# A decoder block with a mixture of experts on one core: the first half's turned blocks laid over the normalised tokens, seven expert numbers in one word, results added in place and the last transfers on two queues

## The reference, cut to what matters

```python
def _moe(x, gate, expert_bias, w1, w2, w3, shared_w1, shared_w2, shared_w3):
    scores = jax.nn.sigmoid(xt @ gate.T)                # 896 tokens, 8 experts
    _, sel = jax.lax.top_k(scores + expert_bias, 2)     # two experts for a token
    order = jnp.argsort(sel.reshape(-1), stable=True)
    ...
    xb = (xt[token_idx] * scores_sorted[:, None]).astype(jnp.bfloat16)
    for e in range(8):
        h = jax.nn.silu(xb @ w1e.T) * (xb @ w3e.T)      # 512 -> 256
        oe = h @ w2e.T                                  # 256 -> 512
        out_r = out_r + jnp.where((expert_ids == e)[:, None], oe, 0.0)
    hs = jax.nn.silu(xt @ shared_w1.T) * (xt @ shared_w3.T)
    out = (hs @ shared_w2.T).at[token_idx].add(out_r)
x = x + _moe(layernorm(x), ...)
```

## Time and profile before

| | us |
|---|---|
| median of 3 runs (lowest, highest) | 639.5 (638.59, 640.96) |
| the profiled execution | 643.89 |
| its span from first to last instruction | 642.1 |
| PE busy in the span | 571.7 (89%) |
| part of the span before `experts` | 517 |
| `experts` | 125 |

### The profile page before, as it was taken

How to read it: one execution, slowest core, us unless ns; L and a number is a source line. 1 busy time by engine, 2 the same in 40 slices (tenths; PEclk the granted TensorE clock), 3 DMA queues, 4 the chain that set the end, 5 groups by cost and what they waited for, 6 DMA issues and landing times. The chain is left out here.

```text
span 642.1 us, 9755 instructions
## 1 busy us (share of the span) xinstructions
PE 571.7 (89%) x3440; PEld 446.8 (70%) x3440; DVE 386.3 (60%) x900; ACT 291.6 (45%) x660; POOL 295.7 (46%) x290
## 2 busy tenths in 40 slices
PE   2768898997989789999999999999999869959995
PEld 1545675665657578888888888888888659923452
DVE  6563678587575676546665566645666478446652
ACT  3133441633735466636764477634776223123320
POOL 0508733641853346613875068631785114615531
PEclk9978897998979989999999999999999975969999
DMA  8853555565724057223533164331500064278434
GB/s 274 213 188 106 187 185 182 181 215 155 281 97 145 2 162 238 40 55 127 132 91 99 62 172 116 66 65 39 192 2 0 1 231 190 84 139 195 140 106 140
DMA packets 52979, 85.00 MB, mean 132 GB/s; under 512 B 25699, under 2 KB 34613, under 8 KB 52037
## 3 DMA queue, kind: packets, MB, share of 16 engines
q1 hardware_dynamic: 50276, 72.47, 36.3%
q0 software_dynamic: 2656, 11.91, 8.2%
HBM read 63.20 MB, written 30.09 MB: 145 GB/s over the span
## 5 line engine op out<-in xcount | busy, mean ns | idle before, releaser
L1448 POOL TENSOR_TENSOR xprob<-xprob,erec 128x375 f32<-128x375 f32 x112 | 90.3, 814 | 136.3 <-DVE erec L1227 136.0
L915 ACT ACTIVATE xprob<-s_ps,nmax 128x375 f32<-128x375 f32 x112 | 64.3, 575 | 59.7 <-DVE nmax L1222 56.9
L1222 DVE TENSOR_REDUCE nmax<-s_ps 128x1 f32<-128x375 f32 x112 | 59.6, 538 | 0.0
L59 PE MATMUL k_ps<-ow,ctx_hl 128*112 128x512 f32 x128 | 52.5, 410 | 2.8 <-DVE ctx_hl L1217 2.1
L1441 POOL TENSOR_TENSOR prob<-prob,rec 112x1792 f32<-112x1792 f32 x8 | 25.5, 3184 | 54.7 <-DVE rec L1163 54.7
L61 PE MATMUL k_ps<-ow,ctx_hl 128*112 128x512 f32 x128 | 50.5, 394 | 0.0
L1217 DVE TENSOR_TENSOR ctx_hl<-k_ps,ctx_hl 128x448 fp32r<-128x448 f32 x32 | 20.0, 625 | 50.6 <-ACT ctx_hl L910 50.6
L60 PE MATMUL k_ps<-ow,ctx_hl 128*112 128x512 f32 x128 | 50.2, 392 | 0.0
L1197 DVE TENSOR_TENSOR pt_hl<-f_ps,pt_hl 125x512 fp32r<-125x512 f32 (+1 forms) x67 | 41.7, 623 | 11.1 <-ACT pt_hl L887 10.2
L59 PE MATMUL s_ps<-kvt,qt_hl 128*128 128x376 f32 x112 | 44.9, 401 | 2.0 <-ACT xprob L915 1.0
L1686 POOL DMA_INDIRECT done_dram<-o_sb,to x28 | 27.1, 969 | 37.1 <-DVE o_sb L1961 21.9
(11 more groups left out here) (238 smaller groups left out, 1523.6 us busy)
## 6 DMA issues: line engine op xcount, KB each, us to landing
ow_raw<-ow_dram SPq DMA_DIRECT2D x16, 512.0 KB, 3.6
w<-w_dram SPq DMA_DIRECT2D x6, 1024.0 KB, 10.3
raw_b<-in_raw SPq DMA_DIRECT2D x8, 640.0 KB, 4.9
raw_m<-in_raw SPq DMA_DIRECT2D x8, 576.0 KB, 4.8
raw_q<-in_raw SPq DMA_DIRECT2D x8, 512.0 KB, 6.5
ow_dram<-bw_sb SPq DMA_DIRECT2D x8, 512.0 KB, 5.6
qw_raw<-aw_dram SPq DMA_DIRECT2D x16, 256.0 KB, 3.5
w_dram<-in_w POOLq DMA_DIRECT2D x8, 512.0 KB, 5.4
```

The costliest lines, as they stand in the source:

```text
L59: pe.matmul(out, a_hl[0], b_hl[0], start=start, stop=False, skip_group_check=True)
L915: act.activation(xprob[z][:, 0:L], s_bank(n, k)[:, 0:L], ACT.Exp, bias=nmax[:, z:z + 1], accum_out=esum[:, z:z + 1]).then_inc(xexp_done, 1)
L1222: dve.tensor_reduce(nmax[:, z:z + 1], s_bank(n, k)[:, 0:L], X, ALU.max, negate=True).then_inc(xmax_done, 1)
L1448: pool.tensor_tensor(xprob[z][:, 0:L], xprob[z][:, 0:L], erec[:, z:z + 1].broadcast_to([128, L]), ALU.mult).then_inc(xp_ready, 1)
```

## The change

Four parts.

1. **Place of the first half's blocks.** `xg` is split: the second half's two chunks stay over `xn2_hl` (`xg_late`), the first half's lie over `fxn`, one chunk over sequences 0 to 3, the other over 4 to 7 (`xg_early`). `load_slots(0)` no longer waits for gu_done; chunk 0 waits for rows_ready at 8 and ft_done at 4, chunk 1 for rows_ready at 16 and ft_done at 8.
2. **Expert numbers.** DVE packs seven numbers of three bits into one word. PE reads a word for every seven blocks and takes a number out with a register division and a remainder.
3. **Buffers and results.** `o_sb` has six buffers. `result` adds into `x_sb`; y_sb and the wait for its stores go away.
4. **Last transfers.** Of the second half's four loads `got` and four stores, those of sequences 5 and 7 are issued by ACT, the others by SP.

```diff
-    SENT, CHUNK = 4, 7
+    SENT, CHUNK = 6, 7
...
+        with ExitStack() as laid:
+            xg_early = []
+            for z in range(CHUNKS):
+                xg_early.append(sb(f"xg_early{z}", [128, KC, CHUNK * 128], BF16, laid))
+                sb(f"xg_gap{z}", [128, HALF * C - KC * CHUNK * 64], F32, laid)
+        xg = [xg_early[0], xg_early[1], xg_late[:, 0], xg_late[:, 1]]
...
-        y_sb = [tile(f"y_sb{z}", [T, C]) for z in range(2)]
...
+        def load_done(eng, h, some):
+            for z in range(SENT):
+                eng.wait_ge(put[z], 16 * put_by((h + 1) * BLOCKS)[z])
+            eng.wait_ge(rows_ready, TOP2 * B)
+            for s in some:
+                src = done_dram[h][0:SPARE].rearrange("(r b t) c -> b t r c", r=TOP2, b=HALF)
+                eng.dma_start(got[:, HALF * h + s], src[s]).then_inc(got_loaded[s], 16)
+
+        def store(eng, b):
+            eng.wait_ge(y_ready, b + 1)
+            eng.dma_start(out[b], x_sb[:, b, :]).then_inc(y_stored[b % 2 if b >= HALF else 0], 16)
...
-                    sp.wait_ge(gu_done, UNITS)
+                    if h:
+                        sp.wait_ge(gu_done, UNITS)
...
+                        if h == 0:
+                            sp.wait_ge(rows_ready, TOP2 * HALF * (z + 1))
+                            sp.wait_ge(t_done, HALF * (z + 1))
+                        sp.dma_start_transpose(xg[CHUNKS * h + z][:, :, :], slots_dram[h][j, 0:C]).then_inc(xg_loaded[CHUNKS * h + z], 16)
...
-                load_done(1)
-                for b in range(HALF, B):
-                    store(b)
+                load_done(sp, 1, range(0, HALF, 2))
+                for b in range(HALF, B, 2):
+                    store(sp, b)
...
-                    return pe.value_load(own_e[0:1, h, j:j + 1], min_val=0, max_val=EXPERTS - 1)
+                    z = g // CHUNK
+                    if len(seven) == z:
+                        pe.wait_ge(own_ready, z // CHUNKS + 1)
+                        seven.append(pe.value_load(own_e[0:1, z // CHUNKS, z % CHUNKS:z % CHUNKS + 1], min_val=0,
+                                                   max_val=EXPERTS ** CHUNK - 1))
+                    return (seven[z] // EXPERTS ** (g % CHUNK)) % EXPERTS
...
+                load_done(act, 1, range(1, HALF, 2))
+                for b in range(HALF + 1, B, 2):
+                    store(act, b)
...
-                    dve.tensor_scalar(own_e[:, h], own_f[:, h], float(EXPERTS - 1), None, ALU.min).then_inc(own_ready, 1)
+                    own.link(dve.tensor_scalar(own_f[:, h], own_f[:, h], float(EXPERTS - 1), None, ALU.min))
+                    of = own_f[:, h, 0:BLOCKS].rearrange("p (z i) -> p z i", z=CHUNKS)
+                    own.link(dve.tensor_copy(packed[:, h], of[:, :, CHUNK - 1]))
+                    for i in reversed(range(CHUNK - 1)):
+                        own.link(dve.scalar_tensor_tensor(packed[:, h], packed[:, h], float(EXPERTS), of[:, :, i], ALU.mult, ALU.add))
+                    dve.tensor_copy(own_e[:, h], packed[:, h]).then_inc(own_ready, 1)
...
-                    wait(dve, y_stored[z], 16 * (b // 2))
-                    dve.tensor_tensor(y_sb[z][:, :], x_sb[:, b, :], sum_ps(b), ALU.add).then_inc(y_ready, 1)
+                    dve.tensor_tensor(x_sb[:, b, :], x_sb[:, b, :], sum_ps(b), ALU.add).then_inc(y_ready, 1)
```

More of the change, by code:

```diff
@@ L107, in build @@
         with ExitStack() as laid:
-            xg = sb("xg", [128, 2 * HALVES, KC, BLOCKS * 64], BF16, laid)
+            xg_late = sb("xg_late", [128, 2, KC, BLOCKS * 64], BF16, laid)
         xn2_hl = sb("xn2_hl", [128, 2, KC, N], F32R)
@@ L134, in build @@
         experts(nc, a, sem, sb, ident, x_sb, xn2_hl, sw_hl, sd_hl, stats_all, dve_chain, chain_end, slots_dram, w13_dram, w2_dram,
-                w_cast, rows_laid, xg, out)
+                w_cast, rows_laid, xg_late, out)
 def attention(nc, a, sem, sb, ctx, ident, x_sb, xn2_hl, w_raw, p_raw, mask, stats_all, ow_dram, kvn_dram, kvt_dram, aw_dram,
@@ L1528, in experts @@
 def experts(nc, a, sem, sb, ident, x_sb, xt_hl, sw_hl, sd_hl, stats_all, dve_chain, chain_end, slots_dram, w13_dram, w2_dram,
-            w_cast, rows_laid, xg, out):
+            w_cast, rows_laid, xg_late, out):
     UNITS = HALVES * HC
     ALL = HALVES * BLOCKS
-    SENT, CHUNK = 4, 7
+    SENT, CHUNK = 6, 7
     CHUNKS = BLOCKS // CHUNK
@@ L1550, in experts @@
         up_sb = [tile(f"up_sb{z}", [128, HID]) for z in range(2)]
-        tile("xt_rest", [128, 2 * KC * 64])
         hid = [tile(f"hid{z}", [128, HID], BF16) for z in range(2)]
@@ L1554, in experts @@
         o_sb = [tile(f"o_sb{z}", [128, C], BF16) for z in range(SENT)]
-        y_sb = [tile(f"y_sb{z}", [T, C]) for z in range(2)]
+        tile("xt_rest", [128, 2 * C])
         gate = tile("gate", [128, KC, EXPERTS])
@@ L1573, in experts @@
         full, own_f, own_e = (tile("full", [1, HALVES, 2 * EXPERTS, EXPERTS]), tile("own_f", [1, HALVES, 2 * EXPERTS]),
-                              tile("own_e", [1, HALVES, 2 * EXPERTS], I32))
+                              tile("own_e", [1, HALVES, CHUNKS], I32))
+        packed = tile("packed", [1, HALVES, CHUNKS])
         token = tile("token", [T, TOP2, HALF], I32)
@@ L1633, in load_slots @@
                             sp.wait_ge(xg_loaded[CHUNKS * h + z - 1], 16)
-                        sp.dma_start_transpose(xg[:, CHUNKS * h + z], slots_dram[h][j, 0:C]).then_inc(xg_loaded[CHUNKS * h + z], 16)
+                        if h == 0:
+                            sp.wait_ge(rows_ready, TOP2 * HALF * (z + 1))
+                            sp.wait_ge(t_done, HALF * (z + 1))
+                        sp.dma_start_transpose(xg[CHUNKS * h + z][:, :, :], slots_dram[h][j, 0:C]).then_inc(xg_loaded[CHUNKS * h + z], 16)
                     sp.dma_start(to[:, h], rows_of[:, :, C:ROW].bitcast(I32)).then_inc(to_loaded[h], 16)
[L1637 to L1648, removed]
                 load_slots(0)
                 load_slots(1)
-                load_done(0)
+                load_done(sp, 0, range(HALF))
                 for b in range(HALF):
-                    store(b)
-                load_done(1)
-                for b in range(HALF, B):
-                    store(b)
-                for z in range(2):
-                    sp.wait_ge(y_stored[z], 16 * (B // 2))
+                    store(sp, b)
+                load_done(sp, 1, range(0, HALF, 2))
+                for b in range(HALF, B, 2):
+                    store(sp, b)
+                sp.wait_ge(y_stored[0], 16 * (HALF + HALF // 2))
+                sp.wait_ge(y_stored[1], 16 * (HALF // 2))
             @block.gpsimd
@@ L1749, in up @@
                     for k in range(KC):
-                        mm = pe.matmul(b_ps[g % 2][:, :], xg[:, g // CHUNK, k, r], w13[:, e, :, k, :], start=(k == 0), stop=(k == KC - 1))
+                        mm = pe.matmul(b_ps[g % 2][:, :], xg[g // CHUNK][:, k, r], w13[:, e, :, k, :], start=(k == 0), stop=(k == KC - 1))
                     mm.then_inc(up_done, 1)
@@ L1799, in _ @@
                 pe.wait_ge(w_loaded, 16 * 6)
+                seven = []
                 owner = [owner_of(0), owner_of(1)]
@@ L1963, in result @@
                 def result(b):
-                    z = b % 2
                     dve.wait_ge(c_done, b + 1)
-                    wait(dve, y_stored[z], 16 * (b // 2))
-                    dve.tensor_tensor(y_sb[z][:, :], x_sb[:, b, :], sum_ps(b), ALU.add).then_inc(y_ready, 1)
+                    dve.tensor_tensor(x_sb[:, b, :], x_sb[:, b, :], sum_ps(b), ALU.add).then_inc(y_ready, 1)
                 for b in range(B):
```

3 lines of the change are left out of this document (removed).

## The result

| | before | after |
|---|---|---|
| median of 4 runs each, us (lowest, highest) | 640.23 (638.59, 641.97) | 630.07 (629.90, 631.06) |
| profiled execution, its span | 643.89, 642.1 | 630.01, 628.2 |

The ratio is 0.9837, interval 0.9806 to 0.9868: 10.2 us sooner.

The account below looks back on a forecast made before the run. PE was taken to wait 7 us for the first blocks' load, then be bound by its sequencer in the loop. Gains of 1.7 (start), 4.8 (loop) and 2.2 (end) sum to 8.7: 639.5 - 8.7 = 630.8 us, range 626.5 to 635.5.

Parts of the forecast that it names:

- the start: From the shared expert's matmuls to step 4: loading the first blocks earlier gains 1.7 us, with the clock falling again.
- the end: Last gathers, results and stores: no store wait gains 1.6 us, two load queues 0.6; sum 2.2, bounds 1.6 and 2.5.
- the base that the forecast started from: Time before the change, 639.5 us: the 4.4 by which the profiled execution exceeded the median, taken off its span of 642.1.
- the rival to which the prediction gave 0.18: Before step 0: PE's idle time is shorter and the clock holds; gain 11.7, time 627.8 us; chance 0.18.
- DVE is free at 568.8: DVE before step 0: the shared hidden layer, lengthened 1.6 us by `owners(1)`, ends at 568.8, so step 0 starts at 569.3.
- an idle time of 5.2 us: PE idle from 564.1 to 569.3 before step 0, longer than 2.8 us, so the clock falls, returning at 575.3.
- The loop: Steps 4 to 20: without the sequencer's reads steps take 1.41 instead of 1.71 us; gain 4.8.
- 1.2 us that I can't explain: Step 6 to 7, which took 2.91 us: its unexplained 1.2 is kept; loop gain 6.0 if it goes too.
- The second queue's 0.6: Last loads: issuing two on ACT's queue takes 0.9 us off the last issue; 0.6 taken as gain.
- The profile as a distortion of the sequencer: PE's loop: recording instructions stretches the sequencer, so reads are nearly free without a profile; 635.2 us; chance 0.14.
- Slow division: PE's sequencer in the loop: register division with remainder costs 1.1 us, steps take 2.36; 648.6 us; chance 0.05.
- the early start is worth nothing: Before step 0: DVE and ACT chain is longer, or scatters slow chunk 0; gain 7.0, time 632.5 us; chance 0.08.

Follow-up runs that it names:

- early_only: Kernel before with only part 1, the first half's blocks over `fxn`; ratio to before 0.9912.
- longer_chain: Kernel after with 16 more small copies of `packed` on DVE behind `owners(1)`, which change no number; ratio to before 0.9923.
- one_queue: Kernel after with all last loads and stores of the second half on SP's queue; ratio to before 0.9903.
- one_queue_2: Repeat of the kernel after with all last transfers on SP's queue, in a later group on another chip; ratio to before 0.9888.
- read_each: Kernel after with one read of `own_e` for each block, as before, and the short `owners`; ratio to before 0.9920.
- before_again: Kernel before, unchanged but for an empty line at its end; ratio to before 0.9984.
- packed_only: Kernel before with only part 2, seven expert numbers packed in a word; ratio to before 0.9969.
- packed_six: Kernel before with parts 2 and 3 (packed numbers, six buffers, results in place), without parts 1 and 4; ratio to before 0.9975.
- after_again: Kernel after, unchanged but for an empty line at its end, timed in a later group; ratio to before 0.9899.

## Why the prediction was right, point by point

The time, 630.07, lies 0.7 us from the forecast of 630.8. That is in good part luck: the start was put far too low, the end too high, and the base that the forecast started from, 639.5, had become 640.23. What happened at the start of after is the rival to which the prediction gave 0.18, and for that it had forecast 627.8.

*The start: 1.7 forecast, 7.5 in the traces, and 5.6 by early_only's ratio.* The mechanism was right: the load was the wait, it could start at 552, and DVE's and ACT's chain is next. Two sizes were wrong, 2.9 us each. The step "DVE is free at 568.8" took its rows from an execution in which silu 2 was 2.8 us late; DVE reached `hid` at 565.93. And then "an idle time of 5.2 us" was 2.34, so the clock held (the rival that I gave 0.18), and steps 0 to 4 took 5.3 instead of 8.2. longer_chain shows the second case with all its numbers. The two errors are one: late signals make the idle time longer, and in one_queue, one_queue_2 and read_each, each with a silu 1.9 to 3.0 us late, the clock fell. And about 1.0 of the 7.5 belongs to part 2: steps 0 to 4 take 5.3 us in after and 6.3 in early_only, whose clock held as well.

*The loop: 4.8 forecast, 5.5 in the trace pair, but some 2 by itself.* That steps are bound by the sequencer's reads, that an undisturbed step without them takes 1.41, and that division costs nothing that shows, is seen in after's rows, and in read_each, which puts the wait back. What the sum lacked is that shorter steps meet the late signals with hardly any slack. With the reads the loop took 27.5 to 28.6 in every trace; without them 23.0, 25.2, 25.7, 26.2, 26.3, 26.9, 28.4, 28.8 and 29.0. The "1.2 us that I can't explain" of step 6 to 7 was one of these hold-ups, at a place where they come back, and I should have asked what it would do to a loop without slack.

*The end: 2.2 forecast, 0.7 in the trace pair.* No wait for a store is left. The tails of the kernels with y_sb are 13.7 to 14.1, those in place on one queue 12.7 to 12.8: about 1.2 instead of 1.6. The second queue's 0.6 was not there: tails 12.5 to 13.4 with it, so the issue time was not what the last load waited for. In after, the clock falls during the last gathers (1.63 us for the last four, 1.17 before); the sum had no term for it.

*The profile as a distortion of the sequencer* (0.14): not settled. After's profiled execution took 630.01 with a median of 630.07, and before's 643.89 lies within what before's runs span in the three groups, 639.4 to 646.9 (61 runs; before_again's ten reach down to 636.9). But the record has a span and a granted clock for every timed execution, so none is known to have run without recording, and the gaps in the record go with the hold-ups. In the medians the cost of the reads shows in packed_only and packed_six alone, 2.0 and 1.6 us, with intervals that begin at 0.3 and 0.2. *Slow division* (0.05) is refuted by its rows, *the early start is worth nothing* (0.08) by early_only.

*Together.* The forecast's sum of 8.7 stands between 10.2 (the first comparison) and 643.59 - 636.66 = 6.9 (after_again; by its ratio 6.5, between 4.2 and 8.8). Parts 1 and 2 alone add up to 5.6 + 2.0 = 7.6. Beside early_only's 0.9912 the whole change has 0.9903, 0.9899 and 0.9888 in one_queue, after_again and one_queue_2: of what lasts, part 1 is the only part whose share is clear of the noise by more than a little.

*Open.* What makes PE's signals come one to three microseconds late. It isn't the semaphore shared with SP, and no run here varied anything else that could cause it. That the recording of the execution causes it is an untested rival, and the gaps in the record speak for it: only the one trace without hold-ups has none. Nor is it known why after's four first runs all lay at 630 and the six of after_again between 634 and 640; their start is equal, and the loop of the one profiled among each differs by 5.4 us. Another chip may be a part of it, but before rose by 3.4 us from the first comparison to that group, and after by 6.6.

## What to carry to other kernels

Where a load waits for memory and not for data, look for memory that dies sooner, and then read the chain behind it, with its own late arrivals: the idle time that is left bears on whether TensorE's clock falls as well. In loops of small matmuls with addresses from registers, count what the sequencer reads; but expect a loop without slack to show every late signal, and don't book the whole difference. A second queue for the last loads cut the issue time and brought the data no sooner here.

## What the runs showed of the hardware that was not expected

- An engine can start one to three microseconds after the modelled end of the matmul it waits for, in some executions, and in the loop at places that come back: silu 2 of before came 2.8 us later than the same one of after, a copy in after_again 2.0 us behind its matmul. In after's loop there was none (longest step 1.59 us).
- A register division by a constant, with the remainder, sits in a register instruction whose median stays 46 ns; the longest was 166.
- The clock fell behind an idle time of 3.82 us only when PE had been working again for 0.6 us: in read_each step 0 starts at 568.24, and the granted clock is half from 568.9 on. So the price of a wait can fall on work that comes after it: 6.9 us for steps 0 to 4 instead of 5.3.
- With two queues (six traces) the first of four loads of 224 KB let its gather start 3.2 to 3.5 us after the first issue and the last group (five of them) 4.8 to 5.1; with one queue (eight traces) 2.8 to 3.1 and 4.7 to 5.0.
